# Attention with a mixture of experts: two products in place of three for the near values, and another order of one batch's work

## The reference

```
scores = stack([einsum('bhnd,bhnd->bhn', q, shift(k, delta)) for delta in OFFSETS]) * scale + pos_bias
alpha  = softmax(scores);   out = sum_i alpha_i * shift(v, delta_i)
x = layernorm(x + (out * sigmoid(x @ Wgate + bgate)) @ Wout + bout)
```

## Time and profile before

| | us |
|---|---|
| median of 3 runs (2097.2 to 2100.86) | 2100.75 |
| profiled execution, its own time | 2102.96 |
| its span, first to last instruction | 2101.2 |
| TensorE busy | 1556.9 (74%) |
| VectorE busy | 962.6 (46%) |
| ScalarE busy | 907.8 (43%) |
| GpSimd busy | 674.4 (32%) |
| TensorE's granted clock, mean share of full | 0.784 |

### The profile page before, as it was taken

One profiled execution on the slowest core, in us unless ns is written; L12 is line 12 of the kernel. 1 busy time (PEld: TensorE's weight loads), 2 busy tenths in 40 slices (PEclk: granted clock), 3 DMA queues, 4 the chain that ended last, 5 costly groups with the idle time before them and its releaser, 6 DMA issues. The chain is left out here.

```text
span 2101.2 us, 76212 instructions
## 1 busy us (share of the span) xinstructions
PE 1556.9 (74%) x33280; PEld 1045.3 (50%) x33280; DVE 962.6 (46%) x1925; ACT 907.8 (43%) x1544; POOL 674.4 (32%) x654
## 2 busy tenths in 40 slices
PE   0455786878777787878787777869676389999980
PEld 0234555545454455545455554545454247667660
DVE  4213354544445444545454454445455255554535
ACT  1232353534443352635254433526343366565626
POOL 4221333323241423333233415243332303232335
PEclk9665787868776786868687767768687689999995
DMA  3374524525251524334252514243330144444328
GB/s 82 63 203 135 107 77 92 103 76 114 74 117 49 114 64 96 82 74 98 63 114 64 115 49 103 64 87 74 66 86 3 45 134 102 98 90 111 66 31 325
DMA packets 220118, 194.80 MB, mean 93 GB/s; under 512 B 66847, under 2 KB 207151, under 8 KB 219648
## 3 DMA queue, kind: packets, MB, share of 16 engines
q1 hardware_dynamic: 204464, 175.11, 33.7%
q0 software_dynamic: 15360, 15.10, 4.5%
HBM read 98.07 MB, written 86.18 MB: 88 GB/s over the span
## 5 line engine op out<-in xcount | busy, mean ns | idle before, releaser
L394 POOL TENSOR_TENSOR p<-p 128x512 f16<-128x512 f32 x96 | 135.9, 1416 | 522.4 <-ACT p L790 522.2
L804 ACT COPY featT<-gp 128x1024 f16<-128x1024 f16 x96 | 93.4, 1032 | 430.4 <-PE gp L539 430.4
L394 DVE TENSOR_TENSOR p<-p 128x512 f16<-128x512 f32 x96 | 86.4, 900 | 293.4 <-ACT p L790 293.0
L546 PE MATMUL gp<-featT,wr 128*128 128x512 f16 x768 | 193.2, 410 | 19.8 <-DVE mT L945 13.6
L622 PE MATMUL o<-v_near,p 128*32 128x34 f16 (+1 forms) x6144 | 161.2, 185 | 33.9 <-issue 31.4
L1385 PE MATMUL up<-rowsT,w 128*128 128x512 f16 x768 | 173.0, 386 | 9.7 <-DVE w L1462 5.3
L622 PEld LDWEIGHTS o<-v_near,p 128*32 128x32 f16 x6144 | 153.7, 98 | 51.0 <-issue 47.9
L1347 POOL DMA_INDIRECT xln<-y,place x64 | 104.8, 1637 | 220.0 <-DVE y L1489 179.4
L789 ACT ACTIVATE p<-st 128x512 f16<-128x512 f32 x192 | 116.7, 608 | 126.1 <-PE st L590 109.4
L1399 PE MATMUL dn<-w,h 128*128 128x256 f16 x1536 | 170.1, 273 | 0.0
L1093 POOL DMA_INDIRECT disp<-y,sidx x128 | 137.9, 1078 | 65.2 <-issue 49.2
(11 more groups left out here) (173 smaller groups left out, 2953.7 us busy)
## 6 DMA issues: line engine op xcount, KB each, us to landing
qk_dram<-qk SPq DMA_DIRECT2D x64, 256.0 KB, 2.5
v_near<-vs SPq DMA_DIRECT2D x224, 66.0 KB
qs<-qk_dram SPq DMA_DIRECT2D x96, 128.0 KB, 4.6
ks<-qk_dram SPq DMA_DIRECT2D x96, 128.0 KB, 7.7
o_dram<-o_far SPq DMA_DIRECT2D x64, 136.0 KB, 5.9
o_back<-o_dram SPq DMA_DIRECT2D x16, 544.0 KB
v_dram<-vs SPq DMA_DIRECT2D x16, 528.0 KB, 3.3
v_far<-v_dram SPq DMA_DIRECT2D x64, 132.0 KB, 3.5
```

Source lines behind the costliest of these rows:

```text
L394: engine.tensor_tensor(p16[:, b, 1, :], p32[:, b, :], p16[:, b, 0, :], ALU.subtract).then_inc(is_split, 1)
L546: last = nc.tensor.matmul(dst, lhs(a, c), rhs(b, c), start=(k == 0), stop=(k == len(todo) - 1))
L804: gp_done(nc.scalar.copy(featT[:, i, :, :].rearrange("f c t -> f (c t)"), bank[:, :].bitcast(F16)), n, stage, PART_OF_T[stage], i)
```

## The change

- **Near values:** high weights times all 33 columns in one product, low weights times the first 17 in a second: two products in place of three. The low part now lands in columns of its own, so a pair fills both banks: `o[0]` for the even heads, `o[1]` for the odd ones.
- **Merge:** two additions (each 8 heads, 17 columns) of the banks' main part and `o_back`, a wait, and two more (16 columns) that add the low part.
- **Waits of `values`:** every near pair waits for the merge of the pair before it, the first near pair for both far copies as before.
- **Slots:** near0 to near3 stand in slots 5, 6, 7, 8 (before: 6, 7, 8, 8), near0 ahead of `outp` w. `outp` t, w, y and `rank` c stand one slot earlier (4, 5, 6, 4), as do `rout` t, h0 and h1 (9, 10, 11). The scatters move from slots 6 and 7 to 11 and 13.
- **Scores of pair 1:** slot 1 in place of 0, so the q,k product's first half stands ahead of them; exponentials and split one slot later too.
- **SP:** the loads of `v_near` stand in slot 4 in place of 1, behind the stack loads and ahead of the store of the far sums.

```diff
-    3: [("rank", "l"), ("proj", "vg1")], 4: [], 5: [("outp", "t"), ("rank", "c")],
-    6: [("outp", "w"), ("maxp", "near0"), ("rank", "s0"), ("rank", "s1")],
-    7: [("rank", "s2"), ("rank", "s3"), ("outp", "y"), ("maxp", "near1")], 8: [("maxp", "near2"), ("maxp", "near3")],
-    9: [("maxp", "far0")], 10: [("maxp", "far1"), ("rout", "t"), ("split", "x")],
-    11: [("maxp", "t"), ("rout", "h0")],
-    12: [("rout", "h1"), ("gate0", "den0"), ("gate0", "inv0")], 13: [("rout", "h2")], 14: [("rout", "h3")], 15: [("feat", "x")],
+    3: [("rank", "l"), ("proj", "vg1")], 4: [("outp", "t"), ("rank", "c")], 5: [("maxp", "near0"), ("outp", "w")],
+    6: [("maxp", "near1"), ("outp", "y")], 7: [("maxp", "near2")], 8: [("maxp", "near3")],
+    9: [("maxp", "far0"), ("rout", "t")], 10: [("maxp", "far1"), ("rout", "h0"), ("split", "x")],
+    11: [("maxp", "t"), ("rout", "h1"), ("rank", "s0"), ("rank", "s1")],
+    12: [("gate0", "den0"), ("gate0", "inv0")], 13: [("rout", "h2"), ("rank", "s2"), ("rank", "s3")], 14: [("rout", "h3")], 15: [("feat", "x")],
...
-SCORES_AT = [-1, 0, 4, 7, 10, 12]
-EXP_AT = [0, 1, 5, 8, 11, 13]
-SPLIT_AT = [1, 2, 6, 9, 12, 14]
+SCORES_AT = [-1, 1, 4, 7, 10, 12]
+EXP_AT = [0, 2, 5, 8, 11, 13]
+SPLIT_AT = [1, 3, 6, 9, 12, 14]
...
-                if h == 1:
+                if h == 4:
...
-                elif k <= FAR_PAIRS + 1:
-                    alone.wait_ge(far_out, n.at(FAR_PAIRS, min(k, FAR_PAIRS)))
+                elif k <= FAR_PAIRS:
+                    alone.wait_ge(far_out, n.at(FAR_PAIRS, k))
                 else:
-                    alone.wait_ge(merged, n.at(TILES, k - FAR_PAIRS - 1))
+                    alone.wait_ge(merged, n.at(TILES, k - FAR_PAIRS))
...
+                            p = lambda a: p16[:, 2 * (k % 2) + e, a, c:c + BLOCK]
+                            if not far:
+                                v = v_near[:, 4 * (k - FAR_PAIRS) + blk, :, 2 * z + e, :]
+                                dst = o[e][:, 0:PAIRS * VW].rearrange("q (u z c) -> q u z c", u=2, c=VW)[quad, :, z, :]
+                                nc.tensor.matmul(dst, p(0), v, start=True, stop=False, skip_group_check=True)
+                                last = nc.tensor.matmul(dst[:, :, 0:OW], p(1), v[:, :, 0:OW], start=False, stop=True, skip_group_check=True)
+                                continue
...
-                nc.vector.tensor_tensor(ob[:, i, :, :].rearrange("q h c -> q (h c)"), o[i % 2][:, 0:H * OW],
-                                        o_back[:, i, :, :].rearrange("q h c -> q (h c)"), ALU.add).then_inc(merged, 1)
+                of_e = lambda t, e: t[:, i, :, :].rearrange("q (u z e) c -> q e u z c", u=2, e=2)[:, e]
+                src = [o[e][:, 0:PAIRS * VW].rearrange("q (u z c) -> q u z c", u=2, c=VW) for e in range(2)]
+                for e in range(2):
+                    last = nc.vector.tensor_tensor(of_e(ob, e), src[e][:, :, :, 0:OW], of_e(o_back, e), ALU.add)
+                last.then_inc(merge_hi, 1)
+                dve.wait_ge(merge_hi, n.at(TILES, i + 1))
+                for e in range(2):
+                    num = of_e(ob, e)[:, :, :, 0:HD]
+                    last = nc.vector.tensor_tensor(num, src[e][:, :, :, OW:VW], num, ALU.add)
+                last.then_inc(merged, 1)
```

## The result

The changed kernel takes 2065.7 us (median of 4 runs, 2064.2 to 2068.6), the kernel before takes 2100.8 beside it: ratio 0.9835 [0.9817, 0.9854]. I had forecast 95 us less, and it is 35 less.

What follows compares the result with a forecast made beforehand. TensorE's order of work, its gaps and the half clock behind them were taken to bound the attention part. Pieces 14.9 + 28.9 + 26.6 + 18.0 = 88.4 against 95.0 us, over 14 batches plus about 3, gave 2006 us, range 1930 to 2110.

Steps and rivals of the forecast that it cites:

- S: The first stack load of a batch, from which times are counted; one batch walked before the change is 95.0 us.
- Near values: Near pairs' value products on TensorE: 64 in place of 96, 1.6 us a pair, 0.7 us less for each of four.
- piece C: First router product to the end of x's transposes: 24.3 us before, forecast 26.6, with 3.0 added for scatter gaps.
- Merge: VectorE's additions: four taking 1.3 us, 0.9 more each; TensorE's new wait in the last pair taken as 0.3.
- Near V and the far sums: Near V's loads behind the stacks end at S + 18.9; the first merge can start at S + 30.
- The slower rival: Far sums return too late for VectorE's first merge: up to 4.6 us slower a batch, 2162 us; chance 0.15.
- Piece B: From near0 of the maximum stage to the first router product: from 34.9 to 28.9 us.
- the second four: GpSimd's later group of four scatters, 5.1 us, forecast to fall on the far scores.
- Piece D: End of x's transposes to the next stack load: 20.05 to 18.0 us, by a shorter wait before the second far scores.
- Not the scatters': Rival: scatters do not cause the near products' gaps; 4.6 us saved a batch, 2034 us; chance 0.11.
- A: Piece from the first stack load to near0 of the maximum stage, waiting for the stacks: forecast 14.9 us.
- Gaps in the worst place: Rival: both scatter groups cost their whole 5.1 us on values and scores, 7.2 more than taken; 2106 us, chance 0.07.

Runs made afterwards that it cites:

- the order alone: The new order with the old three near products and one-instruction merge, against the kernel before: 2074.7 us, 0.9851.
- the repeat: The changed kernel measured once more, unaltered, for noise, against the kernel before: 2068.9 us, 0.9857.
- taking the tables back: The changed kernel with scores, exponentials and split of the second far pair back in their old slots: 2128.1 us, 1.0142 against the kernel before.
- two of three: The kernel before with new near values and merge, and the second far pair's scores, exponentials and split one slot later, in old slots: 2031.0 us, 0.9693.
- The two kernels with later scatters: Scatters one batch later, against the kernel before: with new values in the old order 2021.5 us, 0.9972; with the whole change 2039.8 us, 1.0079.

## Why the prediction was right and wrong

**What bounds it**: right. TensorE's order and the waits in it set the batch; near0 waits for the stacks and starts at S + 14.7 on average (forecast 14.9).

**Near values**: about right. The forecast of 1.6 us for a pair is 1.70 at full clock, a saving of 0.63 for 0.7. I had left out that at half clock it is 2.48. Alone, values and merge give 3.05 us a batch. That is the four pairs' 0.72 each (2.69 to 1.97 us) and nothing for the merges, where my terms net of them gave about half. Of the product times, the Trainium skill's estimate ("TensorE: Matmul & The Clock Gate", section "Back-to-back issue gap"), 1.76, and my 1.6 are both 0.06 to 0.10 off. In the new order the same edit adds only 0.4 us a batch (94.31 against 93.90), which is less than two profiles of one kernel differ by. A pair does get 0.77 us shorter there too (3.50 to 2.73). But in piece C, where two pairs together save 1.8 us, the rest takes it back: C stays at 31.5, with the granted clock at 0.74 in place of 0.78. Why the clock falls there is not shown. That sum was not additive, and I had added.

**Merge**: right, and smaller. Four additions, two each of these groups, are 1.15 us in place of 0.44, 0.7 more for the 0.9 forecast:

```profile
L903 DVE TENSOR_TENSOR ob<-o,o_back 128x136 f32<-128x136 f32 x128 | 32.0, 291 | 118.3 <-PE o L621 93.6 <-DMA o_back<-o_dram 17.5 <-remote 7.1
L908 DVE TENSOR_TENSOR ob<-o,ob 128x128 f32<-128x128 f32 x128 | 31.2, 286 | 2.2
```

The wait for the merge in the last pair is 0.95 us (3.8 in 4), but most of a like wait is there with the old merge too. From the end of VectorE's half of the split to the first product it is 1.08 us in the changed kernel and 0.54 with the order alone, so the new merge adds some 0.5 us, not 0.3. I had hidden it beside GpSimd's split, but both halves of that split are late, VectorE's behind its own reciprocal, and the merge comes after them.

**Near V and the far sums**: the first merge starts at S + 30.4, forecast 30 and, behind y's residual, 31.8. The load back ended VectorE's wait once, in 17.5 us of the row above, at 165.6 us in the first batches; in the repeat it did so five times, 22.3 us in all, of which four were waits of 1.0 to 1.8 us. Near V in its old place changes nothing. The slower rival falls.

**Piece B, 6.0 us less**: the size held (5.1), and the reason only in part. Part by part I had built it from the new order of the stage. But with the scatters put back it is 35.84, the old length, and in the kernel before without scatters it is 29.53 in the old order. So the gain is the scatters' leaving; without them B is even 1.5 us longer in the new order (31.02) than in the old, where the product with Wout is not in it.

**Piece C, 2.3 us more: the step that failed.** It is 8.5 more. Putting the scatters back takes 4.5 of them away, and leaving them out in the changed kernel takes 4.6 (on the other chip). This term was 3.0 in the sum. I had placed the second four on the far scores, but the last pair's values now stand under them, 5.0 us for the forecast 1.6. The other 4.0 I had at nothing. They are there with no scatters in C, in both of those kernels. Most of them come from the router's parts ahead of the transposed maxima: with these back, B + C falls by 3.3. In the walked batch they show as the wait of 1.47 for GpSimd's split, of 1.00 for mT, and as half clock behind: a pair in 2.5 us and h2 with h3 in 6.76 us where I had 5.3. I had listed the products of C with their durations before the change, h1, h2 and h3 at full clock, and no wait for a split or for mT between them. The step that failed is thus the overlap in C: the sum has the splits and mT done by the time TensorE comes to them, and they are not. Over the batches, TensorE idles 3.05 us in C with the scatters put back and 1.56 before, at a granted clock of 0.79 and 0.94. So waits are 1.5 of the 4.0, and the other 2.5 are longer busy time at the lower clock. In the changed kernel it idles 5.7 us at 0.74.

**Piece D, 2.05 us less**: right in kind, too small. It is 5.6 less, and 4.8 less by taking the tables back. I had bounded the wait at 1 to 4 us and priced only the wait; the tables also take the scores themselves out of the way of the q,k product.

**Not the scatters'**: the rival falls as to the gaps. The near gaps are 18.3 us in 500 with scatters beside them, 1.2 without, and in other kernels stand at the values, the scores or the transposes, wherever the scatters stand. That they come to about 5 us a batch, as the forecast had it, is borne out by B in the kernel before (35.86 with, 29.53 without), with the chip's difference in it. The Trainium skill ("SBUF — State Buffer", section "SBUF: two separate sides") has TensorE's own port wait for nobody, and its rule would have moved nothing out of B; B lost 5.1 to 6.3 us. By which path a scatter starves TensorE of small products no run here shows.

**Together**: by the profiles, values -3.05, tables -2.8 in the old slots and -4.8 in the new, new slots +3.3 to +5.3. The forecast took the new slots for a gain of several microseconds. By pieces, the forecast of -6.6 misses 6.2 in C, 0.9 in B and 0.5 in A, and D gives 3.5 more than I had: -2.6, and 14 times that is 36 us, the measured difference. "Gaps in the worst place" put 7.2 on C, close in size, but half of what C lost is not the scatters'.

## What to carry to other kernels

Walk a moved stage product by product with the waits between them, and ask of each wait what clock the work behind it gets; a sum of durations at full clock hides both. Put indirect DMAs of GpSimd beside long products or a wait that exists anyway, hold them there with a wait on that place, and keep them from in front of a split on which TensorE waits. Before a reorder of several parts is kept, take each part back alone: here two of three gave the gain (0.9693) and the third took half of it back.

## What the runs showed of the hardware

- Under indirect DMAs issued by GpSimd, TensorE's small products come in groups some 0.73 us apart with gaps of 0.4 to 0.5 us. The 24 products of 512 columns from 745.30 in the changed kernel, beside three scatters, show no such gaps.
- An indirect DMA takes GpSimd 0.97 us alone and 4.55 us beside VectorE's 2.30 us mT, two hid operations and one on og. It ends 0.85 us behind the last of these (746.96), and the next one takes 0.96 us beside the reciprocal. It is not peculiar to indirect DMAs: in the changed kernel without scatters, GpSimd's split stands in that place (733.98) and takes 4.02 us in place of 1.18. The split of 512 elements on VectorE is 0.68 alone and 1.84 beside GpSimd's split (750.26 against 699.93 in the changed kernel). For this the Trainium skill (same page and section) has the rule of one shared pair of ports, held by one of the two for a whole instruction, with a warning that the descriptors of such a DMA can't be written meanwhile. The trace agrees in kind, with two differences. The 4.55 us span four VectorE instructions, and GpSimd did not get in between them. And of the operations outside the two-port modes the section names those with two operands in SBUF, while one of mT's is in PSUM: GpSimd's split was held beside mT all the same, for it still needed 1.02 of its 1.18 us when the operation on og ended.
- The same kernel before takes 2100 to 2105 us on two chips and 2026 on a third. The two kernels with later scatters that ran on the third gained nothing there (0.997, 1.008). They did not run on the others, and the changed kernel did not run whole on the third, so whether a ratio moves with the chip is not shown. Why the third is faster is open.
